# Attention scores per head on half of TensorE's rows, without zeros in the query stacks

## Time and profile before

| what | before |
|---|---|
| median of 3 runs | 1128.78 us (1128.32 to 1128.98) |
| span of the profiled execution | 1128.8 us |
| TensorE matmul busy | 1004.9 us, 89% |
| TensorE weight load busy | 610.1 us, 54% |
| VectorE busy | 863.1 us, 76% |
| ScalarE busy | 672.0 us, 60% |
| GpSimd busy | 556.0 us, 49% |
| mean granted TensorE clock | 0.983 of 2.4 GHz |

### The profile page before, as it was taken

The page is one execution under the profiler, slowest core; times in us unless marked ns, Lnnn a source line. Parts: engine busy times, 40 slices in busy tenths (PEclk is TensorE's granted clock), DMA queues, the critical chain, the costliest instruction groups (busy, mean ns, idle before and its releaser), DMA issues.

```text
span 1128.8 us, 23960 instructions
## 1 busy us (share of the span) xinstructions
PE 1004.9 (89%) x7578; PEld 610.1 (54%) x7672; DVE 863.1 (76%) x2054; ACT 672.0 (60%) x998; POOL 556.0 (49%) x783
## 2 busy tenths in 40 slices
PE   4679999999998999899998999989899899999987
PEld 2234746556473555646555474655646456564635
DVE  7668788878878787798877879867888778787626
ACT  3126666657575565656656566555756557575665
POOL 6515374545536454373535537445363535536263
PEclk9689999999999999999999999999999999999999
DMA  5730515114051421405123050511405123050000
GB/s 125 163 66 1 133 28 116 45 66 88 10 134 29 104 57 57 87 20 116 44 80 74 11 135 26 116 47 55 87 21 127 35 81 80 8 125 20 19 19 10
DMA packets 86413, 75.18 MB, mean 67 GB/s; under 512 B 9425, under 2 KB 80018, under 8 KB 86290
## 3 DMA queue, kind: packets, MB, share of 16 engines
q1 hardware_dynamic: 84210, 72.78, 27.4%
q10 hardware_dynamic: 2080, 0.79, 0.3%
HBM read 36.33 MB, written 30.15 MB: 59 GB/s over the span
## 4 chain that ended last, share of the span: by engine, by line
PE 52%; DVE 19%; issue 15%; POOL 8%; ACT 2%; DMA 2%; DVEq 1%; SPq 0%; POOLq 0%; another core or an unknown queue 0%; ACTq 0%
DVE mx L1023 8%; PE ps L522 7%; PE ps L504 7%; PE ps L507 6%; POOL h L1231 5%; PE ps L701 5%; PE ps L662 5%; PE ps L488 5%; PE ps L641 4%; PE ps L539 3%; PE ps L534 2%; DVE xn L880 2%; POOL r L1174 2%; PE ps L556 1%; PE ps L608 1%
## 5 line engine op out<-in xcount | busy, mean ns | idle before, releaser
L1023 DVE TENSOR_REDUCE mx<-ps 128x2 f32<-128x512 f32 (+1 forms) x512 | 306.5, 616 | 65.0 <-PE ps L507 59.5
L778 ACT ACTIVATE pt<-ps 128x1024 f32<-128x1024 f32 (+1 forms) x256 | 233.1, 916 | 164.5 <-PE ps L488 162.7
L1184 POOL TENSOR_SCALAR_AFFINE_SELECT pt<-pt 128x512 f32<-128x512 f32 x256 | 169.7, 663 | 289.8 <-ACT pt L778 289.8
L504 PE MATMUL ps<-kd,qz 128*128 128x256 bf16 (+1 forms) x1024 | 188.3, 267 | 32.6 <-DVE mx L1023 25.2
L504 PEld LDWEIGHTS ps<-kd,qz 128*128 128x128 bf16 x1024 | 75.7, 99 | 188.9 <-DVE mx L1023 94.9
L507 PE MATMUL ps<-mask,identb 128*128 128x512 bf16 (+1 forms) x450 | 158.9, 354 | 0.0
L488 PE MATMUL ps<-qz,kd 128*128 128x512 bf16 (+1 forms) x512 | 142.6, 361 | 14.8 <-issue 11.5
L641 PEld LDWEIGHTS ps<-m,act_t 128*128 128x128 f32 x1024 | 127.9, 191 | 48.8 <-DVE act_t L1110 31.2
L522 PE MATMUL ps<-pt,va 128*32 128x256 f32 (+1 forms) x2048 | 146.2, 364 | 7.9 <-ACT ot L783 2.0
L641 PE MATMUL ps<-m,act_t 128*128 128x128 f32 x1024 | 141.9, 281 | 9.3 <-DVE act_t L1110 9.3
L824 ACT ACTIVATE lin<-ps,mbias 128x512 f32<-128x512 f32 x128 | 87.8, 686 | 76.7 <-PE ps L636 42.3
(11 more groups left out here) (154 smaller groups left out, 1592.2 us busy)
## 6 DMA issues: line engine op xcount, KB each, us to landing
qz<-qk_parts SPq DMA_DIRECT2D x32, 384.0 KB
kd<-qk_parts SPq DMA_DIRECT2D x32, 384.0 KB
qk_parts<-qp SPq DMA_DIRECT2D x16, 384.0 KB, 2.4
qk_parts<-kp SPq DMA_DIRECT2D x16, 384.0 KB, 2.6
xl<-L_attn_x SPq DMA_DIRECT2D x16, 256.0 KB, 3.1
qk_parts<-qp SPq DMA_DIRECT2D x16, 256.0 KB, 2.7
qk_parts<-kp SPq DMA_DIRECT2D x16, 256.0 KB, 2.9
xnr<-xn SPq DMA_DIRECT2D x16, 256.0 KB, 2.8
```

Of the source, the lines that this page charges most:

```text
L504: nc.tensor.matmul(o[:, par, lo:], qz[q][:, p, par, P * i:P * (i + 1)], kd[q][:, p, P * (i - 1) + lo:P * (i + 1)], start=par == 0, stop=False,
L778: nc.scalar.activation(pt[:, n % NPT, :, 0:w_q], src, ACT.Exp, scale=SCALE).then_inc(exp_ok.sem, 1)
L1023: nc.vector.tensor_reduce(mx[:, i, h:h + 2], src, AX.X, ALU.max).then_inc(mx_ok.sem, 1)
L1184: sel1 = nc.gpsimd.affine_select(out=pt[:, s, :, 0:P], in_=pt[:, s, :, 0:P], compare_op=ALU.is_ge, fill=0.0, base=0, pattern=[[0, HG], [1, ...
```

## The change

Each head's scores become a matmul of its own over its own rows: 51 rows (48 and the shift) in the second pass, 48 in the first. The array is then used in two halves of 64 rows. `score` and `score_t` are called from one function, `scores(b, q, n, half)`, which sends the first pass of one half (par = half) and the second pass of the other (par = 1 - half) by turns: score pr 0, score_t pr 0, score pr 1, score_t pr 1, and then the mask. `values` of chunk n-3 still stand between the two halves. Banks now belong to par and not to pr. The semaphore that tells ScalarE that a chunk of the second pass is there (`sT_ps`) is raised at the end of half 1, and both waits of a half (exp of chunk n-2, maxima of the bank) stand ahead of its first matmul. `qz` loses its second copy and its zeros: no zeros are written to it at the start, and the two transfers from `zrow` of each batch go away.

```diff
-SHIFT = 6 * DH
+QK = 6 * DH
+ROWS = QK + NPART
...
-        qz = [sb(f"qz{i}", [P, NPAIR, 2, T], BF16) for i in range(2)]
+        qz = [sb(f"qz{i}", [P, NPAIR, T], BF16) for i in range(2)]
...
-            (kd[0][:].rearrange("p n t -> p (n t)").bitcast(F32), two_ones), (zrow[:], 0.0), (cp[:], 0.0),
-            (qz[0][:], 0.0), (st[:], 0.0),
+            (kd[0][:].rearrange("p n t -> p (n t)").bitcast(F32), two_ones), (cp[:], 0.0), (st[:], 0.0),
...
-
-                        sp.dma_start(qz[q][first + SHIFT:first + SHIFT + NPART, :, par],
-                                     zrow[:].unsqueeze(1).to_broadcast([NPART, NPAIR, T])).then_inc(stacks_in.sem, 16)
-                        for n, dst in enumerate((qz[q][first:first + SHIFT, :, par], kd[q][first:first + SHIFT])):
+                        for n, dst in enumerate((qz[q][first:first + QK], kd[q][first:first + QK])):
...
+            def score_t(b, q, n, par, pr):
                 g, j = n // NT, n % NT
...
                 w_q = 2 * P if j < NT - 1 else P
...
+                rows = slice(64 * par, 64 * par + ROWS)
+                return nc.tensor.matmul(bank(2 * (n % 2) + par)[:, 2 * P * pr:2 * P * pr + w_q],
+                                        kd[q][rows, 2 * g + pr, P * j:P * (j + 1)],
+                                        qz[q][rows, 2 * g + pr, P * j:P * j + w_q], start=True, stop=True)
+
+            def score(b, q, n, par, pr):
                 g, i = n // NT, n % NT
...
                 lo = 0 if i else P
...
+                rows = slice(64 * par, 64 * par + QK)
+                nc.tensor.matmul(bank(4 + par)[:, 2 * P * pr + lo:2 * P * (pr + 1)],
+                                 qz[q][rows, 2 * g + pr, P * i:P * (i + 1)],
+                                 kd[q][rows, 2 * g + pr, P * (i - 1) + lo:P * (i + 1)], start=pr == 0, stop=False,
+                                 skip_group_check=True)
+
+            def score_mask(n, par):
+                lo = 0 if n % NT else P
+                o = bank(4 + par).rearrange("p (r k) -> p r k", r=2)
                 nc.tensor.matmul(o[:, :, lo:], identb[:], mask[:, :, lo:], start=False, stop=True,
                                  skip_group_check=True).then_inc(s_ps.sem, 1)
+
+            def scores(b, q, n, half):
+
+                main, nxt = has(b), has(b + 1)
+                if main and half == 0:
+                    if n == 0:
+                        pe.wait_ge(*done(stacks_in, b))
+                        pe.wait_ge(*done(shift_in, b))
+                    if n >= 2:
+                        pe.wait_ge(*done(exp_ok, b, n - 1))
...
+                if nxt:
+                    if n == 0 and half == 0:
...
+                    else:
+                        pe.wait_ge(*done(mx_ok, b + 1, 2 * n - 1 + half))
+                for pr in range(2):
+                    if nxt:
+                        score(b + 1, 1 - q, n, half, pr)
+                    if main:
+                        mm = score_t(b, q, n, 1 - half, pr)
+                if main and half == 1:
+                    mm.then_inc(sT_ps.sem, 1)
+                if nxt:
+                    score_mask(n, half)
...
-                    if main and n < NCH:
-                        score_t(b, q, n)
-                    if nxt and n < NCH:
-                        score(b + 1, 1 - q, n, 0)
+                    if n < NCH:
+                        scores(b, q, n, 0)
                     if main and 3 <= n < NCH + 3:
                         values(b, q, n - 3)
-                    if nxt and n < NCH:
-                        score(b + 1, 1 - q, n, 1)
+                    if n < NCH:
+                        scores(b, q, n, 1)
...
-                            h = HG * g + 2 * pr
-                            nc.vector.tensor_reduce(mx[:, i, h:h + 2], src, AX.X, ALU.max).then_inc(mx_ok.sem, 1)
+                            nc.vector.tensor_reduce(mx[:, i, HG * g + pr:HG * (g + 1):2], src, AX.X, ALU.max).then_inc(mx_ok.sem, 1)
...
-                        nc.gpsimd.memset(qz[1][:], 0.0).then_inc(stacks_set.sem, 1)
```

More of the change, by code:

```diff
@@ L470, in _ @@
             pe.wait_ge(weights_in.sem, 16 * len(WEIGHTS))
-            def score_t(b, q, n):
+            def score_t(b, q, n, par, pr):
                 g, j = n // NT, n % NT
-                if n == 0:
-                    pe.wait_ge(*done(stacks_in, b))
-                    pe.wait_ge(*done(shift_in, b))
-                if n >= 2:
-                    pe.wait_ge(*done(exp_ok, b, n - 1))
-                else:
-                    pe.wait_ge(*done(hid_ok, b - 1))
-                    if isinstance(b, int) and b == 0:
-                        for s in (st_ok, qkr_ok, v_ok):
-                            pe.wait_ge(*done(s, b + 1))
-                w_q = 2 * P if j < NT - 1 else P
-                for pr in range(2):
-                    p = 2 * g + pr
-                    o = bank(2 * (n % 2) + pr).rearrange("p (r q) -> p r q", r=2)[:, :, 0:w_q]
-                    mm = nc.tensor.matmul(o, kd[q][:, p, P * j:P * (j + 1)], qz[q][:, p, :, P * j:P * j + w_q],
-                                          start=True, stop=True)
-                mm.then_inc(sT_ps.sem, 1)
@@ L492, in score @@
-            def score(b, q, n, pr):
-                g, i = n // NT, n % NT
-                if n == 0:
-                    pe.wait_ge(*done(stacks_in, b))
-                    pe.wait_ge(*done(gc_ok, b - 2, E))
-                    pe.wait_ge(*done(gpre_ok, b))
-                else:
-                    pe.wait_ge(*done(mx_ok, b, 2 * n - 1 + pr))
-                lo = 0 if i else P
-                o = bank(4 + pr).rearrange("p (r k) -> p r k", r=2)
-                p = 2 * g + pr
-                for par in range(2):
-                    nc.tensor.matmul(o[:, par, lo:], qz[q][:, p, par, P * i:P * (i + 1)],
-                                     kd[q][:, p, P * (i - 1) + lo:P * (i + 1)], start=par == 0, stop=False,
-                                     skip_group_check=True)
+                w_q = 2 * P if j < NT - 1 else P
@@ L944, in _ @@
                 nc.vector.memset(dst, value).then_inc(blank_set.sem, 1)
[L945 removed]
+                if n == 1:
                     norm_x(0, 0, (0, 1))
```

18 lines of the change are left out of this document (12 added, 6 removed).

## The result

The kernel after takes 1219.06 us, the median of 4 runs (1213.02 to 1219.89), against 1128.79 us for the kernel before in the same session: 1.0789 of it, with a 95% interval of 1.0765 to 1.0814. That is 90 us slower, outside of the range of 1104 to 1188. The ratios in this document are those of mean times (to 0.1%), without runs over 1.5% above the fastest of their kernel, which count as slow: there is one each in the experiments "Overlap taken away", "A filler" (on the kernel after) and "Rows against mode", and in the first two it is the one profiled.

A forecast was written before the change was run, and what follows sets the result against it. In the score stretch TensorE (28.25 of 30.40 us) and VectorE (27.47) were taken to bound the kernel. 1128.8 + 37.5 (2.5 a batch) + 2.2 + 1 - 1.7 = 1167.8, taken as 1168 us (+3.5%), range 1104 to 1188.

The forecast's parts named there:

- The streaming saved: Score chunks: both passes side by side on different halves save 0.43 us a full chunk, 1.28 a group of four.
- The changes of mode: Score chunks: five changes of tiling mode in place of two, 0.12 us each, adding 1.44 us a group of four chunks.
- The second half's start: Score chunks: a pair of matmuls takes 0.03 us a half beyond its bare 0.213, adding 0.24 us a group.
- TensorE's own work: Chunks 4 to 13: sum for TensorE +0.40 us a group, +1.2 a batch for three groups.
- The copy's wait: `values` of chunks 4, 8 and 12 newly wait 0.74 us for the copy `ot`; +1.1 us a batch after softening.
- The merged waits: Chunks 0 to 3: both passes now wait for the maxima, +0.2 us a batch (0 to 0.5).
- b = -1: First pass alone at the start: a change of mode ahead of each mask, 0.14 x 16, +2.2 us.
- the zero transfers: Start of the kernel: two transfers on SyncE, 0.93 and 0.77 us, go away, -1.7 us once.
- b = 15: Last step, second pass alone, split round `values`, ScalarE setting the pace: +1 us (0 to 3).
- The free change of mode: Rival: a change to halves of rows costs next to nothing, so the kernel is faster, 1100 to 1110 us; chance 0.25.
- The second rival: The halves don't overlap, nothing is saved and mode changes come on top: 5.3 us a batch, 1210 us; chance 0.07.
- Cancelling: Rival: gains and prices cancel, a change near 0.05 us, copy's wait swallowed by VectorE's waits: 1127 to 1131 us; chance 0.05.

The follow-up runs named there:

- Overlap taken away: Kernel after with both passes of a half sent to the same 64 rows, so pairs stream one after another: 1330.3 and 1389.6 us.
- A filler: An unused matmul of 128 rows and 512 columns added where TensorE waits: 1221.11 us on the kernel after, 1130.77 us on the kernel before.
- Rows against mode: Kernel before with rows 0 to 64 in place of 128 in both passes, no change of mode added: 1181.52 us, 1.0438.
- full rows in the new order: Kernel before, all 128 rows and zeros kept, with its work in the order of the kernel after: 1164.1 us, 1.0321.
- the moved side work: VectorE's other work put behind half 0's readings: second pass ahead on kernel after 1188.81 us, with only second pass halved 1132.6; control, kernel before, 1146.24.
- half rows in the old order: Kernel after's half rows in the order of the kernel before, second pass of a chunk first: 1225.58 us, 1.0875.
- the mask first: Kernel after with the mask ahead of the pairs in half 1, four changes of mode a chunk in place of five: 1206.14 us, 1.0694.
- T ahead: Kernel after with the second pass (T) of chunk n+1 beside the first pass of chunk n: 1204.03 us, 1.0635.
- half of the columns alone: Kernel before, full 128 rows, with half of the columns of each score matmul in both passes: 1113.23 us, 0.987.
- halves of T alone: Kernel before with only the second pass (T) as half-row matmuls, behind `values`, one chunk ahead: 1147.78 us, 1.017.
- halves of T ahead with the side work moved: Kernel before with the second pass (T) in half rows a chunk ahead, VectorE's other work behind half 0's readings: 1132.6 us, 1.0038.

## Why the prediction was right or wrong

**The direction was right, the size was not, and its main cause was in no step.** The part of the 90 us that the order of the work made is some 25: 1.5 us for each of 15 stretches, and 2.6 at b = 15 (as in the kernel with full rows in the new order). The clock took the rest, some 60 us: 44 in the stretches (66.6 less 22), some 7 at b = 15, and most of the 9.2 ahead of the first second pass. The order tried alone cost more than 25, namely 36 us (1164.1 against 1128.0), with 10 us more at half clock than the kernel before; by that the clock's share is 54. How far the two causes act on each other was not separated further.

*The failing step:* the prediction took "at 2.4 GHz (the granted clock of this stretch is 1.00)" from the kernel before and kept it for the kernel after. The clock was no term of the sum and none of the rivals, and no reason was given for leaving it out, though the change gives each score matmul 48 or 51 rows in place of 128. In the kernel after the clock fell to half in 12 of 15 stretches, ahead of b = 0 and at b = 15: 228 us in place of 41, worth 54 to 60 of the 90 us.

*The streaming saved* (1.28 us a group): right; four matmuls of a half and the change behind them take 0.32 us.

*The changes of mode:* five a chunk at 0.116 us, taken at 0.12. Right. The Trainium skill has it that such a switch drains TensorE ("TensorEngine Tiling (Array Packing)", section "Key Properties"); for halves of rows the trace agrees, with 0.32 us from pairs to mask where the columns take 0.21.

*The second half's start* (+0.24 a group): wrong, it is nothing; pairs start within 0.01 us. That agrees with the some 4 ns of the Trainium skill ("TensorE: Matmul & The Clock Gate", Part 3).

*TensorE's own work* thus is 0.05 us shorter in a group (7.46: four times 1.86, less 0.21 for the narrow S and mask and 0.21 for the narrow `values`, plus 0.44 for the turn), and not 0.40 longer. Forecast +1.2 a batch, worked out from the trace -0.15. A full chunk was to take 2.1 to 2.2 us and takes 1.86.

*The copy's wait:* seen as foretold ("<- ACT ot", 0.53 us in chunk 7, where 0.74 was forecast), but in one of the three places a batch and not in all: 7.7 us in b = 1 to 14, 0.5 a batch, and three waits of 1.47 at b = 15. In the stretches it was worth nothing: with it gone they took 32.7 us, not less. Forecast +1.1 a batch.

*The merged waits* (+0.2 in chunks 0 to 3): wrong. They took 6.52 us (297.93 to 304.45 of b = 3), less than the 6.72 of the earlier trace rows. (The prediction says that `values` has not begun in them; `values` of chunk 0 stands in chunk 3.)

*What was there instead:* from chunk 4 to `values` of chunk 13 it is 25.8 us, 22.4 of work and 3.4 of waits, against 22.5 and 1.5 before.

```profile
297.93 0.23 PE L480 MATMUL ps<-kd,qz 48*128 48x128 bf16 x1
...
304.45 0.23 PE L480 MATMUL ps<-kd,qz 48*128 48x128 bf16 x1
...
330.23 0.64 PE L534 MATMUL ps<-pt,va 128*32 128x256 f32 x8
```

The waits grew by 1.9 us, 0.5 of them for the copy and the rest for maxima. Masks now come at 1.22 and 0.64 us; that VectorE's fixed order doesn't fit these distances is what the moved side work speaks for and its control against. The sum of the prediction, +2.5 a batch, stood near the measured +1.5 by terms that were mostly others.

*b = -1* (+2.2 less 1.7 for the zero transfers, so +0.5): 9.2 us. The clock was low for 55 us there in place of 22. With 65 rows in the full mode, where no change of mode is added, it was low for 47 us and 5.2 us were lost. Whether the transfers' 1.7 us were gained was not tried alone.

*b = 15* (+1): 9.8 us, of which 2.6 the order (as with full rows in the new order) and the rest, by difference, the clock, low for 26 us.

*The rivals.* The free change of mode (1100 to 1110) failed with the price of 0.116 us. The second rival, no overlap, came near the time with its 1210, by a mechanism that did not occur: the pairs overlap. Cancelling (1127 to 1131) failed as well, though TensorE's own work did cancel.

**What stays open.** A filler of full rows brought back 14 of the 187 us of added low clock in its profiled run and some 40 in the median one; what mix of rows would hold the clock was not found. And rows act together with columns and order: half rows in the old order had 265 us low, in the new one 228 (183 with the mask first, 193 with T ahead), half of the columns alone 79, halves of T alone 49. Only times of one profile each stand behind these figures, and the kernels with few rows scatter. No version that computes all of the scores beat the kernel before: the nearest are halves of T ahead with the side work moved, +0.4%, and the kernel before with the filler, +0.16% (1.0007 to 1.0026).

## What to carry to other kernels

Before a matmul is cut to fewer rows of the array, the granted clock of the profile is a term of the sum: here the rows of zeros were no plain waste. With them TensorE kept its full clock nearly all of the time, and taking them away cost more than the streaming saved. Where two engines hand chunks to each other, look at the distances at which results come, and at what the other engine has placed between them: with 1.10 and 0.87 us a stretch took 30.8 us, and the other orders, some with less work for TensorE, took 31.5 to 33.0. Moving VectorE's side work gave 0.8 and 1.1 us back in two of them and cost 1.4 in the first, so such a move is tried and not assumed. And a wait that a change adds need not cost its length: in the stretches, where TensorE also waits for VectorE, taking it away again gave nothing.

## What the runs showed of the hardware that was not expected

- The number of rows that matmuls drive moves the granted clock: with 65 rows in place of 128 and the same instructions, columns and order (but one head's data of two left out) 0.908 to 0.930 against 0.980 to 0.987, and 1181.5 against 1128.6 us; with one half at a time 0.81 to 0.86 and up to 1389.6 us.
- Matmuls on the two row halves start within 0.01 us and run side by side; a change between full mode, row halves and column strips costs 0.116 us in the mean of five.
- Runs of the kernels whose matmuls drive few rows scatter more: 1330.3 and 1389.6 us for one, at mean clocks of 0.861 and 0.809, and 1169.8 to 1189.5 for the 65 rows, where the full rows in the new order gave 1163.5 and 1164.7.
